# Attention with two value banks taken in turn, each head's value products as one stream, and VectorE exponentials for heads 0 and 2 in turn

## What is computed

```python
scores = jnp.einsum('bhqd,bhkd->bhqk', q, k) / np.sqrt(HEAD_DIM)
attn = jax.nn.softmax(scores, axis=-1)
out = jnp.einsum('bhqk,bhkd->bhqd', attn, v)
x = _layernorm(x + out.transpose(0, 3, 2, 1).reshape(b, s, 256) @ Wo + bo)
x = _layernorm(x + ffn(x))     # ffn: (silu(x@w_gate*s_gate) * (x@w_up*s_up)) @ w_down * s_down
```

## Time and profile before

| | us |
|---|---|
| median of 3 runs (lowest to highest) | 604.43 (603.85 to 604.56) |
| the profiled execution, device time | 603.95 |
| its span, first to last instruction | 601.8 |
| TensorE busy | 589.7 |
| weight loads of TensorE busy | 249.9 |
| ScalarE busy | 508.9 |
| VectorE busy | 419.7 |
| GpSimd busy | 54.4 |

### The profile page before, as it was taken

The page is one execution under the profiler, slowest core; times in us unless marked ns, Lnnn a source line. Parts: engine busy times, 40 slices in busy tenths (PEclk is TensorE's granted clock), DMA queues, the critical chain, the costliest instruction groups (busy, mean ns, idle before and its releaser), DMA issues.

```text
span 601.8 us, 10478 instructions
## 1 busy us (share of the span) xinstructions
PE 589.7 (98%) x3952; PEld 249.9 (42%) x3952; DVE 419.7 (70%) x772; ACT 508.9 (85%) x614; POOL 54.4 (9%) x51
## 2 busy tenths in 40 slices
PE   8999999999999999999999999999999999999994
PEld 7883222222222232222232232222323227988974
DVE  6671006889898767697676668888767696686875
ACT  4549999999999999999999999999999995163351
POOL 7606000000000000000000000003000001102021
PEclk9999999999999999999999999999999999999998
DMA  9567884211112010101211010112010000101102
GB/s 212 88 105 89 120 114 89 35 22 24 31 36 42 8 33 5 33 13 29 58 19 28 11 28 11 29 32 46 7 32 7 8 4 9 39 2 35 36 1 70
DMA packets 36184, 24.70 MB, mean 41 GB/s; under 512 B 24930, under 2 KB 30946, under 8 KB 35538
## 3 DMA queue, kind: packets, MB, share of 16 engines
q1 hardware_dynamic: 34932, 23.42, 22.9%
q10 hardware_dynamic: 1200, 0.59, 0.4%
HBM read 6.56 MB, written 4.33 MB: 18 GB/s over the span
## 4 chain that ended last, share of the span: by engine, by line
PE 84%; SPq 8%; DVE 2%; DMA 2%; ACT 1%; issue 1%; ACTq 0%; POOLq 0%; POOL 0%; DVEq 0%
PE ps L1238 38%; PE ps L1210 26%; PE ps L1347 10%; PE ps L1324 4%; SPq L389 4%; PE ps L1080 3%; PE ps L1260 3%; SPq L391 2%; SPq L399 1%; DMA k_stack<-k_part 1%; DMA x_tok<-in_L_attn_X 1%; DVE attn_q L800 1%; PE ps L1278 1%; SPq L378 1%; PE ps L1066 1%
## 5 line engine op out<-in xcount | busy, mean ns | idle before, releaser
L641 ACT ACTIVATE probs<-ps 128x1024 f32<-128x1024 f32 (+1 forms) x512 | 446.4, 1109 | 15.3 <-PE ps L1210 14.8
L1238 PE MATMUL ps<-probs,v_all 128*17 128x512 f32 x1926 | 269.1, 598 | 1.2 <-DVE attn_q L800 0.5
L1210 PE MATMUL ps<-q_slot,k_stack 51*128 51x512 f32 x1024 | 200.0, 460 | 0.8 <-DVE bits L868 0.8
L1210 PEld LDWEIGHTS ps<-q_slot,k_stack 51*128 51x128 f32 x1024 | 85.4, 184 | 223.2 <-ACT probs L641 209.6
L868 DVE TENSOR_SCALAR bits<-ps 128x512 int32<-128x512 f32 x61 | 42.0, 689 | 52.7 <-PE ps L1210 35.5
L660 ACT ACTIVATE sg<-ps,sgate_c 128x512 f32<-128x512 f32 x32 | 22.1, 689 | 49.5 <-PE ps L1347 49.5
L1238 PE MATMUL ps<-poly,v_all 128*17 128x512 f32 x122 | 63.1, 599 | 0.0
L800 DVE COPY attn_q<-ps 128x512 f32<-128x512 f32 x16 | 11.1, 692 | 69.9 <-PE ps L1238 69.9
L1238 PEld LDWEIGHTS ps<-probs,v_all 128*17 128x17 f32 x1926 | 33.6, 95 | 62.2 <-issue 51.5
L892 DVE SCALAR_TENSOR_TENSOR poly<-poly,bits 128x512 f32<-128x512 f32 x61 | 43.7, 717 | 6.3
L888 DVE SCALAR_TENSOR_TENSOR poly<-poly,mant 128x512 f32<-128x512 f32 x61 | 42.2, 692 | 2.1
(11 more groups left out here) (99 smaller groups left out, 451.6 us busy)
## 6 DMA issues: line engine op xcount, KB each, us to landing
q_slot<-qy SPq DMA_DIRECT2D x64, 64.0 KB
k_stack<-k_part SPq DMA_DIRECT2D x12, 256.0 KB
at_dram<-attn_q SPq DMA_DIRECT2D x64, 34.0 KB
at<-at_dram SPq DMA_DIRECT2D x8, 272.0 KB, 2.9
q_slot<-qy SPq DMA_DIRECT2D x64, 32.0 KB
x_tok<-in_L_attn_X SPq DMA_DIRECT2D x14, 128.0 KB, 5.7
k_stack<-k_part SPq DMA_DIRECT2D x12, 128.0 KB
out<-out_tmp SPq DMA_DIRECT2D x12, 128.0 KB, 2.2
```

What stands on the lines that cost most here:

```text
L641: nc.scalar.activation(probs[:, slot_of(g), first:2, :].rearrange("p a b -> p (a b)"), ps[:, 2 * ring + first:2 * ring + 2, :].rearrange(" ...
L1210: last = nc.tensor.matmul(ps[:, 2 * ring + half, :], k_stack[s % QUADS][base:base + ROWS, p, kt * P:(kt + 1) * P], q_slot[slot][base:base ...
L1238: last = nc.tensor.matmul(ps[32 * hh:32 * hh + VW, ACC, :], v_all[:, tiles[hh], NQ * (s % QUADS) + hh, :], prob, start=(kt == 0), stop=(kt ...
```

## The change

Banks 6 and 7 now take the steps in turn: step s sums its value products in `ACC[s % 2]`. The order of the products is no longer written per step but per head, as one list over all 256 positions (`value_order(hh)`), so that a head's products run on over a step's end. VectorE takes head 0 (of the even pair) and head 2 (of the odd pair) in turn, always three positions behind (`BEHIND`). The tiles it takes are new, 64 in all instead of 61. The first product of a step waits for the saving of the step before the last. The output projection and the transposes write to whichever of the two banks is not summing, move to other units (8 and 12 in stage 1, 5 and 11 in stage 2, 5 and 10 in stage 0), and wait until that bank has been saved. VectorE's other work moves among the chains: `save_attn(s-1)` goes behind the step's first chain, `ln1_add` behind the fourth of stages 1 and 2.

```diff
-ACC = 6
+ACC = (6, 7)
...
-FFN_BANK = 7
...
-    return FFN_BANK if c < LAST else 1 + 2 * b
+    return ACC[b] if c < LAST else 1 + 2 * b
...
-    return FFN_BANK if c < LAST - 1 else 2 * ko
+    return ACC[1] if c < LAST - 1 else 2 * ko
...
-    return [] if s == 0 else [10, 13] if s == 1 else [2, 5, 8, 11, 14] if s in (2, 3, 4) else [2, 6, 10, 13]
-def value_order(s):
-    behind = ({2: 4, 5: 7, 8: 10, 11: 13, 14: 15} if len(poly_tiles(s)) == 5 else {2: 5, 6: 9, 10: 12, 13: 15})
-    late = {behind[kt]: kt for kt in poly_tiles(s)}
-    others = [kt for kt in range(UPS) if kt not in poly_tiles(s)]
-    return [late[i] if i in late else others.pop(0) for i in range(UPS)]
+    if s < 2:
+        return [] if s == 0 else [10, 13]
+    if s <= QUADS:
+        return [0, 3, 6, 10, 13]
+    return ([0, 4, 8, 12], [0, 5, 9, 12], [0, 4, 7, 10, 13], [0, 4, 8, 12])[s % QUADS]
+BEHIND = 3
...
-ORDER = [value_order(s) for s in range(STEPS)]
-BY_POLY = [2 * (UPS * s + kt) for s in range(STEPS) for kt in poly_tiles(s)]
-POLY_NO = {g: n for n, g in enumerate(BY_POLY)}
-def poly_products(g):
-    s, kt = g // 2 // UPS, g // 2 % UPS
-    return UPS * s + ORDER[s].index(kt) + 1
+UNITS = UPS * STEPS
+BY_POLY = [(UPS * s + kt) for s in range(STEPS) for kt in poly_tiles(s)]
+POLY_HEAD = {u: 2 * (n % 2) for n, u in enumerate(BY_POLY)}
+def value_order(hh):
+    late = {u + BEHIND: u for u in BY_POLY if POLY_HEAD[u] == hh}
+    others = [u for u in range(UNITS) if POLY_HEAD.get(u) != hh]
+    return [late[i] if i in late else others.pop(0) for i in range(UNITS)]
+ORDER = [value_order(hh) for hh in range(NQ)]
+POSITION = [{u: i for i, u in enumerate(order)} for order in ORDER]
+POLY_NO = {2 * u + POLY_HEAD[u] // 2: n for n, u in enumerate(BY_POLY)}
+def first_product(s):
+    return min(POSITION[hh][u] for hh in range(NQ) for u in range(UPS * s, UPS * (s + 1)))
+def last_product(s):
+    return max(POSITION[hh][u] for hh in range(NQ) for u in range(UPS * s, UPS * (s + 1)))
+STARTS = {first_product(s): s for s in range(STEPS)}
+def poly_products(n):
+    return POSITION[POLY_HEAD[BY_POLY[n]]][BY_POLY[n]] + 1
...
-    return g // 2 + 1
+    heads = [hh for hh in (g % 2 * 2, g % 2 * 2 + 1) if not (g in POLY_NO and hh == POLY_HEAD[g // 2])]
+    return max(POSITION[hh][g // 2] for hh in heads) + 1
...
-        dve.wait_ge(pv_done, UPS * (s + 1))
+        dve.wait_ge(pv_done, last_product(s) + 1)
...
-        nc.vector.tensor_copy(attn_q[s % 2][:], ps[:, ACC, :].rearrange("p (u r) -> p r u", r=HD)
+        nc.vector.tensor_copy(attn_q[s % 2][:], ps[:, ACC[s % 2], :].rearrange("p (u r) -> p r u", r=HD)
...
-        g = BY_POLY[n]
+        g = 2 * BY_POLY[n] + POLY_HEAD[BY_POLY[n]] // 2
...
-            dve.wait_ge(pv_done, poly_products(BY_POLY[n - RESULTS]))
+            dve.wait_ge(pv_done, poly_products(n - RESULTS))
...
-        c = s // QUADS - 1
-        if s:
-            save_attn(s - 1)
-        tiles = [POLY_NO[2 * (UPS * s + kt)] for kt in poly_tiles(s)]
-        stage = s % QUADS
+        c, stage = s // QUADS - 1, s % QUADS
+        tiles = [BY_POLY.index(UPS * s + kt) for kt in poly_tiles(s)]
...
+            if s:
+                save_attn(0)
...
+        save_attn(s - 1)
...
-        if c >= 0 and stage == 2:
-            ln1_add(c, 0)
...
-            ln1_add(c, 1)
+            ln1_stats(c)
+        exponentials(tiles[1])
+        if c >= 0 and stage == 3:
+            ln1_variance(c)
...
-        exponentials(tiles[1])
+        exponentials(tiles[2])
...
-            ln1_stats(c)
+            ln1_scale(c)
...
-        exponentials(tiles[2])
-        if c >= 0 and stage == 3:
-            ln1_variance(c)
-        for n in tiles[3:]:
+        exponentials(tiles[3])
+        if c >= 0 and stage in (1, 2):
+            ln1_add(c, stage - 1)
+        for n in tiles[4:]:
...
-        if c >= 0 and stage == 3:
-            ln1_scale(c)
...
-        s, kt = u // UPS, u % UPS
...
-        elif kt == 0:
-            pe.wait_ge(attn_saved, s)
-        tiles = [ORDER[s][kt], kt, kt, kt]
-        pairs = [2 * (UPS * s + tiles[hh]) + hh // 2 for hh in range(NQ)]
-        pe.wait_ge(exp_done, 1 + max(pairs[i] for i in range(NQ) if i or pairs[0] not in POLY_NO))
-        if pairs[0] in POLY_NO:
-            pe.wait_ge(poly_done, POLY_NO[pairs[0]] + 1)
+        if u in STARTS:
+            begun = STARTS[u]
+            before, stage = begun // QUADS - 1, begun % QUADS
+            if begun >= 2:
+                pe.wait_ge(attn_saved, begun - 1)
+            if before >= 1 and stage == 1:
+                pe.wait_ge(yt_ready, KO * before)
+            if before >= 0 and stage in (2, 3):
+                pe.wait_ge(ln1_sum, 2 * before + stage - 1)
+        tiles = [ORDER[hh][u] for hh in range(NQ)]
+        pairs = [2 * tiles[hh] + hh // 2 for hh in range(NQ)]
+        by_poly = [POLY_HEAD.get(tiles[hh]) == hh for hh in range(NQ)]
+        pe.wait_ge(exp_done, 1 + max(pairs[hh] for hh in range(NQ) if not by_poly[hh]))
+        if True in by_poly:
+            pe.wait_ge(poly_done, max(POLY_NO[pairs[hh]] for hh in range(NQ) if by_poly[hh]) + 1)
...
-            g = pairs[hh]
-            if hh == 0 and g in POLY_NO:
+            g, t = pairs[hh], tiles[hh]
+            s, order = t // UPS, POSITION[hh]
+            if by_poly[hh]:
...
-            last = nc.tensor.matmul(ps[32 * hh:32 * hh + VW, ACC, :],
-                                    v_all[:, tiles[hh], NQ * (s % QUADS) + hh, :],
-                                    prob, start=(kt == 0), stop=(kt == TT - 1))
+            places = [order[i] for i in range(UPS * s, UPS * (s + 1))]
+            last = nc.tensor.matmul(ps[32 * hh:32 * hh + VW, ACC[s % 2], :],
+                                    v_all[:, t % UPS, NQ * (s % QUADS) + hh, :],
+                                    prob, start=(u == min(places)), stop=(u == max(places)))
...
-        elif j == 0 and c:
-            pe.wait_ge(yt_ready, KO * c)
-        if j == 2 and c < LAST:
-            pe.wait_ge(ln1_sum, 2 * c + 1)
+        elif j in (0, 2) and c < LAST:
+            pe.wait_ge(attn_saved, QUADS * (c + 1) + 1 + j // 2)
...
+            if c < LAST - 1:
+                pe.wait_ge(attn_saved, QUADS * (c + 2))
...
-    UNITS = UPS * STEPS
+    OUT_AT, TURN_AT = {1: (8, 12), 2: (5, 11)}, (5, 10)
...
-        if c >= 0 and stage in (1, 2) and kt in (8, 15):
-            project_out(c, 2 * (stage - 1) + kt // 15)
-        if c >= 1 and stage == 0 and kt in (3, 8):
-            turn_y(c - 1, kt // 8)
+        if c >= 0 and stage in (1, 2) and kt in OUT_AT[stage]:
+            project_out(c, 2 * (stage - 1) + OUT_AT[stage].index(kt))
+        if c >= 1 and stage == 0 and kt in TURN_AT:
+            turn_y(c - 1, TURN_AT.index(kt))
```

## The result

The changed kernel takes 616.17 us (median of 4 runs, 615.82 to 618.85) against 604.49 (four runs now): 1.0208 times as long, interval 1.0182 to 1.0235, 11.7 us slower. I had said 613.0, range 605 to 618: right in direction and in its cause, the later wait, and 3.2 us short.

The account below looks back on a forecast made before the run. ScalarE bounds steps like 2 to 4, TensorE those with projections or transposes. Step losses 2.2 + 2.5 + 1.9 + 1.3 + 1.0 = +8.9 us on 603.95 gave 612.9, stated as 613.0 us, range 605 to 618.

Parts of the forecast that it names:

- Head 2's later exponential: Units holding back head 2's product: it waits one exponential later, costing between 0 and 14 us over 29 half exponentials.
- VectorE's chains are late: Rival, steps from 2 on: late readings delay scores, adding 4 to 7 us, 617 to 620 us; chance 0.07.
- The rival that TensorE has room: Attention: the new wait is hidden and steps fall to their floors, -3.4 us, 600.5 us; chance 0.15.
- The price of a place: Each half exponential within three successive units holding back head 2's product, 29 in all: 0.3 us each.
- half, held-back head and projection in one unit: Unit 12 of steps 5 and 13: the three coincide and cost 1.37 us; these steps +0.8 us each.
- Step 9, the one I walked in full: Losses of 0.31, 0.95, 0.31 and 1.00 us, 29.75 us against 28.82: +0.9 us.
- the steps that I did by analogy: Steps 6, 10, 14: +0.6 us each; 7, 11, 15: +0.45 each; 8 and 12: +0.5 each.
- one or two places each: Steps 7, 11 and 15: that many half exponentials hit by the later wait, +0.45 us per step.
- two of 0.3 and two small losses of 0.1: Step 10, counted with 6 and 14: losses 0.3, 0.9, 0.1, 0.3, 0.95, 0.1; +0.6 us each.
- the gain I had put into the sum: Six projection and two transpose steps: products no longer wait for VectorE's copy at step start, at most -1.7 us.
- Moves: Saving, layer-norm additions, query loads, GpSimd's power and projection waits in new places: all free, no cost.
- What stands behind the wait: TensorE's queue: the next scores, needed by ScalarE 0.54 us after they start, start at 259.66 instead of 259.17.

Follow-up runs that it names:

- head0_behind2: Changed kernel with VectorE always taking head 0 and held-back products two positions behind instead of three; 604.84 us, ratio 1.0005.
- wait_only: Kernel before, only products at three positions for every second VectorE tile also wait for the next unit's odd-pair exponential; 614.73 us, ratio 1.0166.
- moves_only: Kernel before with only the projections, transposes and VectorE's additions and copies of them moved as in the change; 609.63 us, ratio 1.0102.
- head0_all: Changed kernel with VectorE always taking head 0, still three positions behind; 629.62 us, ratio 1.0404.

## Why the prediction was right, and where it was short

**Head 2's later exponential: right, and shown from both sides.** The wait alone adds 9.7 us to the kernel before; without it (and with a distance of two) the changed kernel is back within 0.5 us. The alternative that VectorE's chains are late falls: head0_behind2 has the same 64 chains. The rival that TensorE has room falls too: in wait_only a wait of some tenths of a microsecond per unit, and no work, cost 1.7%. By the rule of the Trainium skill ("Perfetto Trace Analysis", "Identifying the Most-Contended Engine"), which judges TensorE's headroom by the busy share of its weight loads and by the share of peak FLOP/s reached, the 42% of its weight loads leave it headroom. The trace does not bear that out here.

**The price of a place: right in the steps that ScalarE bounds; the sum over the other steps was too small.** I took 0.3 us a place, 0.28 in steps 2 to 4, where I counted 2.60 us from one completion to another against 2.31. The place above takes 2.60 by that count (from 140.06 to 141.64 + 1.02 = 142.66), and its 8 places made steps 2 to 4 longer by 2.4 us, 0.30 each. From start to start I had 0.32, with 1.02 us for the exponential that the products wait for, its length right after ScalarE was idle, and noted that it grows in a streak. In the place above it began 0.90 us after 138.04 and ended at 140.06, 1.12 us, and the place cost 0.42: my 0.32 and the 0.10 that it is longer. In 27 of the 29 places the two gaps behind the half are 0.27 to 0.46 us too long together (mean 0.38), those of 0.41 and more all with exponentials of 1.12 to 1.17 us; in the other two, in steps 5 and 13, it is 1.4 us, where I had 1.37 for half, held-back head and projection in one unit. Step 9, the one I walked in full, lacks 0.36, 1.07, 0.27 and 0.98 us where I had 0.31, 0.95, 0.31 and 1.00.

By groups: steps 2 to 4 +2.4 for +2.2; 5, 9 and 13 +3.0 for +2.5; 6, 10 and 14 +2.6 for +1.9 (three times 0.6 is 1.8); 7, 11 and 15 +1.8 for +1.3; 8 and 12 +1.7 for +1.0. So most of what is missing lies in the steps that I did by analogy. In 7, 11 and 15 it was the count: I wrote "one or two places each", the lists give two each, and 6 x 0.30 = 1.8 us is what they grew by. Steps 7 and 15, before and then after (11 stands in the rows of both):

```profile
242.78:270.24 27.46, 27.46 (x32) 1.00 0.13 19
469.17:496.97 27.80, 27.80 (x32) 1.00 0.05 6
```

```profile
250.02:278.07 28.05, 27.71 (x33) 1.00 0.13 20
483.30:511.61 28.31, 27.97 (x33) 1.00 0.05 6
```

Step 10 likewise has three places (0.36, 0.31 and 0.32 us) where I had two of 0.3 and two small losses of 0.1. In steps 8 and 12 two places and the transposes cost 0.3 to 0.4 us more than I had put down for them.

**The two banks: the gain I had put into the sum is not to be seen.** The wait for the copy did go, but in head0_behind2 step 10 is 328.67 to 357.40, 28.7 us, against 28.8 before, steps 8 and 12 are at 28.1 to 28.2 as before, and steps 5, 9 and 13 are 0.4 to 0.5 longer. Steps 2 to 4 gain nothing, as said. That the moves eat the rest is argued: moves_only shows that they cost, but in the one-bank kernel.

**Moves: wrong to cost them at nothing.** In moves_only attention (first exponential to last) is 3.7 us longer than before, of which step 13 has 1.8 and the casts 1.4. I had looked at when each wait is met, not at what lead the piece of work meets, nor at what GpSimd does meanwhile. How much of it is in the changed kernel no run isolates. head0_behind2 carries all the moves and its steps 2 to 15 are 1.0 us longer than before, so with two banks it is less; wait_only and the change differ by 1.4 us.

**What stands behind the wait: my reading was too narrow.** I had named the next scores, queued behind the waiting products. Exchanging the two, even with a buffer more, wins nothing (617.62 us against 616.26 for its control). What the runs allow: TensorE starts each held-back unit's chain one exponential later and can regain 0.16 us per unit, whichever of its two jobs comes first. That this lost time is the cost, and not the order, is an argument from the unit's lengths; no run shows it by itself.

## What to carry to other kernels

Where two engines hand work to each other through a short ring and both are near full, count for every wait which completion of the other engine it names, and compare it with the one already waited for: one further on took slack in 96 units here, and it cost about 0.4 us wherever a short piece of work of the other engine fell into them. When a reordering lets one stream run ahead, list the largest index that any position asks for; overlapping windows (head0_all) raise it silently. A wait that is seen to vanish is not yet time gained: the 5.8 us of waits for the copy are gone in head0_behind2, and its time is that of the kernel before.

## What was not expected of the hardware

VectorE instructions of 0.69 us took 2.26 and 2.19 us while GpSimd cast 128x2048 weights; with the casts moved, the stretched one moved with them. Both read two SBUF tensors. An instruction with a single input was stretched too: in the changed kernel L891 took 1.49 us instead of 0.43, while L888, which reads PSUM, kept its 0.69 beside the same casts:

```profile
423.81 0.69 DVE L888 TENSOR_SCALAR bits<-ps 128x512 int32<-128x512 f32 x1 [2.37 <-PE ps L1229]
424.53 1.49 DVE L891 TENSOR_SCALAR mant<-bits 128x512 int32<-128x512 int32 x1
...
422.01 1.89 POOL L583 CAST wg<-gate 128x2048 fp32r<-128x2048 int8 x1 [42.05 <-PE ps L1229]
423.85 1.89 POOL L584 CAST wu<-up 128x2048 fp32r<-128x2048 int8 x1
```

The Trainium skill, "GPSIMD Engine Reference", section "1. Specifications", says that GpSimd shares its SBUF interfaces with VectorE and contends with instructions that have two SBUF inputs or run in a 2-port performance mode. The trace agrees for the two inputs; whether L891 ran in such a mode no row shows.

In the changed kernel's profiled execution TensorE's granted clock fell to its lower level, 1.2 of 2.4 GHz, once within attention, in step 1, after the 1.90 us in which it waited for VectorE. In that stretch eight products take 1.91 us instead of 1.05:

```profile
99.02 1.91 PE L1267 MATMUL ps<-probs,v_all 128*17 128x512 f32 x8
```

In the profiled execution of head0_behind2, with a wait of 1.0 us at that point, the clock did not fall there.
